# A ViT tower kernel: the pixels' matmuls read x in fp32 instead of two fp16 halves, and x gets two buffers

## What is computed

```
x   = features.reshape(b, c, h, 4, w, 4)
reduce_feats = x.mean((3, 5))                  # mean of each 4 x 4 window
unf = the 16 pixels of each window
q   = layernorm(reduce_feats) @ Wq.T
kv  = layernorm(unf) @ Wkv.T                   # keys and values of 16 pixels
attn  = softmax(q . k over the 16 pixels)      # 8 heads
h   = reduce_feats + (attn . v) @ proj_w.T + proj_b
h   = layernorm(h + lightning_attention(h))    # chunks of 128 tokens, 2 per image
h   = layernorm(h + mixture_of_experts(h))     # top 2 of 8 experts
```

## Time and profile before

| | us |
|---|---|
| median of 3 runs | 3554.83 |
| lowest and highest run | 3554.74, 3558.14 |
| the profiled execution | 3556.12 |
| its span, first to last instruction | 3554.4 |

### The profile page before, as it was taken

One profiled execution on the slowest core, in us unless ns is written; L12 is line 12 of the kernel. 1 busy time (PEld: TensorE's weight loads), 2 busy tenths in 40 slices (PEclk: granted clock), 3 DMA queues, 4 the chain that ended last, 5 costly groups with the idle time before them and its releaser, 6 DMA issues. The chain is left out here.

```text
span 3554.4 us, 81784 instructions
## 1 busy us (share of the span) xinstructions
PE 2747.4 (77%) x22377; PEld 2048.2 (58%) x22377; DVE 2923.7 (82%) x5409; ACT 2049.6 (58%) x12141; POOL 1723.9 (49%) x1661
## 2 busy tenths in 40 slices
PE   3777777777777777777777777777777775399998
PEld 2566666666666666666666666666666655344443
DVE  4999999999999999999999999999999971555554
ACT  3666666666666666666666666666666633244443
POOL 3655555555555555555555555555555520011111
PEclk9999999999999999999999999999999985599999
DMA  2222222222222222222222222222222200000000
GB/s 53 49 49 47 47 47 47 47 47 47 47 47 47 47 47 47 47 47 47 47 47 47 47 47 47 47 47 47 47 47 47 47 1 5 0 16 21 18 21 21
DMA packets 573515, 144.04 MB, mean 41 GB/s; under 512 B 573472, under 2 KB 573472, under 8 KB 573472
## 3 DMA queue, kind: packets, MB, share of 16 engines
q1 hardware_dynamic: 573472, 143.51, 20.6%
HBM read 135.08 MB, written 8.39 MB: 40 GB/s over the span
## 5 line engine op out<-in xcount | busy, mean ns | idle before, releaser
L457 ACT ACTIVATE ps<-ps 128x64 f32<-128x64 f32 x4352 | 935.1, 245 | 848.5 <-PE ps L329 848.3
L607 POOL TENSOR_TENSOR pv<-vs,aw 128x512 f32<-128x512 f32 x512 | 547.1, 1098 | 1178.6 <-DVE aw L781 1178.6
L457 ACT ACTIVATION_READ_ACCUMULATOR ps<-ps 128x1 f32 x4352 | 823.0, 199 | 0.0
L378 PE MATMUL ps<-sm,vpad 128*128 128x128 f32 x4096 | 571.3, 283 | 215.5 <-DVE sm L693 214.6
L378 PEld LDWEIGHTS ps<-sm,vpad 128*128 128x128 f32 x4096 | 511.2, 193 | 303.7 <-DVE sm L693 265.3
L324 PE MATMUL ps<-w_h,xh 128*128 128x128 f16 x2048 | 476.1, 232 | 257.6 <-DVE kq L682 245.7
L329 PE MATMUL ps<-w_h,xl 128*128 128x256 f16 x2048 | 586.7, 286 | 0.0
L327 PE MATMUL ps<-w_h,xh 128*128 128x256 f16 x2048 | 585.3, 286 | 0.0
L324 PEld LDWEIGHTS ps<-w_h,xh 128*128 128x128 f16 x2048 | 237.9, 116 | 492.3 <-issue 348.1
L709 DVE TENSOR_REDUCE agg<-pv 128x128 f32<-128x2048 f32 x128 | 479.6, 3747 | 0.0
L693 DVE TENSOR_TENSOR sm<-ps,decay 128x512 f32<-128x512 f32 x512 | 348.5, 682 | 150.6 <-PE ps L366 150.6
(11 more groups left out here) (222 smaller groups left out, 5971.0 us busy)
## 6 DMA issues: line engine op xcount, KB each, us to landing
xb<-in_x_dram SPq DMA_DIRECT2D x512, 256.0 KB, 4.2
out_dram<-outb SPq DMA_DIRECT2D x128, 64.0 KB, 1.6
w1p<-in_L_ffn_w_dram SPq DMA_DIRECT2D x16, 16.0 KB
b2v<-in_L_ffn_b_dram SPq DMA_DIRECT2D x16, 2.0 KB
w2p<-in_L_ffn_w_dram SPq DMA_DIRECT2D x8, 16.0 KB
b1p<-in_L_ffn_b_dram SPq DMA_DIRECT2D x8, 0.2 KB
sm<-in_L_tok_Wkv_dram SPq DMA_DIRECT2D x4, 16.0 KB, 1.9
w_avki<-in_L_attn_w_qkv_dram SPq DMA_DIRECT2D x4, 16.0 KB, 2.8
```

The costliest lines, as they stand in the source:

```text
L378: mm = nc.tensor.matmul(B7[:, 0:P], vpad[:, s, j * P:(j + 1) * P], sm[:, j * P:(j + 1) * P], start=(j == 0), stop=(j == SL - 1 and s == 0))
L457: return nc.scalar.activation(src if to is None else to, src, ACT.Square, accum_out=dst)
L607: ins = nc.gpsimd.tensor_tensor(pv[:, at].rearrange("p (k d) -> p k d", d=D), vs[:, o, at].rearrange("p (k d) -> p k d", d=D), aw[:, j * W ...
```

## The change

- The tiles `xh`, `xl`, `w_h` and `w_l`, the semaphores `hi_done` and `lo_done`, and all that fills them are gone: `high` on ACT, the subtraction on DVE, the one on POOL, and two set-up instructions on DVE.
- `xb` has two buffers, one for each s.
- A pixel's six fp16 matmuls (four with 128 columns, two with 256) become two fp32 ones, of 128 and 256 columns, with x of `xb` as the stationary operand and `w_ckv` as the moving one.
- `two_pixels(0)` waits for the DMAs of its own unit. `load` waits for `grp` of all units up to two back: PE's last pixel of unit u-2 must be done before x of unit u is fetched.

```
-            xb = sb1("xb", [P, PX])
-            xh = sb1("xh", [P, 2, PX], F16)
-            xl = sb1("xl", [P, 2, PX], F16)
+            xb = sb1("xb", [P, 2, PX])
...
                 def load(i, s):
 
-                    sp.wait_ge(lo_done, done(i, s, 1, 2))
+                    sp.wait_ge(grp, done(i, s, 2, NS))
...
                         if j == 0:
-                            pe.wait_ge(lo_done, done(i, s, 0, 2))
-                            pe.wait_ge(hi_done, done(i, s, 0, 2))
+                            pe.wait_ge(x_in[s], 16 * ST * (i + 1))
...
-                            h, l = xhv[:, n // ST, n % ST], xlv[:, n // ST, n % ST]
-                            nc.tensor.matmul(key, h, w_h[:, 2 * P:3 * P], start=True, stop=False)
-                            nc.tensor.matmul(key, h, w_l[:, 2 * P:3 * P], start=False, stop=False)
-                            nc.tensor.matmul(key, l, w_h[:, 2 * P:3 * P], start=False, stop=True)
-                            nc.tensor.matmul(cv, h, w_h[:, 0:2 * P], start=True, stop=False)
-                            nc.tensor.matmul(cv[:, P:2 * P], h, w_l[:, P:2 * P], start=False, stop=False)
-                            mm = nc.tensor.matmul(cv, l, w_h[:, 0:2 * P], start=False, stop=True)
+                            px = xv[:, n // ST, n % ST]
+                            nc.tensor.matmul(key, px, w_ckv[:, 2 * P:3 * P], start=True, stop=True)
+                            mm = nc.tensor.matmul(cv, px, w_ckv[:, 0:2 * P], start=True, stop=True)
...
-                            at = slice(half * PX // 2, (half + 1) * PX // 2)
-                            nc.scalar.activation(xh[:, o, at], xb[:, at], ACT.Copy).then_inc(hi_done, 1)
...
-                        at = slice(PX // 2, PX)
-                        nc.gpsimd.tensor_tensor(xl[:, o, at], xb[:, at], xh[:, o, at],
-                                                ALU.subtract).then_inc(lo_done, 1)
...
-                        at = slice(0, PX // 2)
-                        V.tensor_tensor(xl[:, o, at], xb[:, at], xh[:, o, at],
-                                        ALU.subtract).then_inc(lo_done, 1)
```

More of the change, by code:

```diff
@@ L102, in vit_tower_kernel @@
         w_ckv = sb("w_ckv", [P, 3 * P])
-        w_h = sb("w_h", [P, 3 * P], F16)
-        w_l = sb("w_l", [P, 3 * P], F16)
         w_qc = sb("w_qc", [P, 2 * P])
@@ L195, in vit_tower_kernel @@
             x_in = [sem("x_in0"), sem("x_in1")]
-            hi_done = sem("hi_done")
-            lo_done = sem("lo_done")
             grp = sem("grp")
@@ L275, in load @@
                 def load(i, s):
-                    sp.wait_ge(lo_done, done(i, s, 1, 2))
+                    sp.wait_ge(grp, done(i, s, 2, NS))
                     for b in range(ST):
-                        sp.dma_start(xb[:, b * PX // ST:(b + 1) * PX // ST].rearrange("p (a w) -> p a w", w=WW),
+                        sp.dma_start(xb[:, s, b * PX // ST:(b + 1) * PX // ST].rearrange("p (a w) -> p a w", w=WW),
                                      xr[bass.ds(i * P, P), s, :, b, :]).then_inc(x_in[s], 16)
@@ L302, in step @@
                     o = 1 - s
-                    xhv = xh[:, s, :].rearrange("p (b k d) -> p b d k", b=ST, d=ST)
-                    xlv = xl[:, s, :].rearrange("p (b k d) -> p b d k", b=ST, d=ST)
+                    xv = xb[:, s, :].rearrange("p (b k d) -> p b d k", b=ST, d=ST)
                     def two_pixels(j):
@@ L474, in pixels_values @@
                                              cvw[:, :, P:2 * P], ACT.Copy).then_inc(cv_done, 1)
[L476 to L480, removed]
-                            at = slice(half * PX // 2, (half + 1) * PX // 2)
-                            nc.scalar.activation(xh[:, o, at], xb[:, at], ACT.Copy).then_inc(hi_done, 1)
                     pixels_values(0)
-                    high(0)
-                    high(1)
                     if there(i, s, 3):
@@ L572, in step @@
                         pool.wait_ge(xs_done, done(i, s, 0, 1))
-                        nc.gpsimd.tensor_tensor(xt[:, 0:PX // 4], xb[:, 0:PX // 4], xb[:, PX // 2:3 * PX // 4], ALU.add)
-                        link(nc.gpsimd.tensor_tensor(xt[:, PX // 4:PX // 2], xb[:, PX // 4:PX // 2],
-                                                     xb[:, 3 * PX // 4:PX], ALU.add))
+                        nc.gpsimd.tensor_tensor(xt[:, 0:PX // 4], xb[:, o, 0:PX // 4], xb[:, o, PX // 2:3 * PX // 4],
+                                                ALU.add)
+                        link(nc.gpsimd.tensor_tensor(xt[:, PX // 4:PX // 2], xb[:, o, PX // 4:PX // 2],
+                                                     xb[:, o, 3 * PX // 4:PX], ALU.add))
                         link(nc.gpsimd.tensor_tensor(xt[:, 0:PX // 4], xt[:, 0:PX // 4], xt[:, PX // 4:PX // 2],
@@ L582, in step @@
                         nc.gpsimd.tensor_tensor(red[:], xp[:, 0, :], xp[:, 1, :], ALU.add).then_inc(xs_done, 1)
-                        pool.wait_ge(hi_done, done(i, s, -1, 2))
-                        at = slice(PX // 2, PX)
-                        nc.gpsimd.tensor_tensor(xl[:, o, at], xb[:, at], xh[:, o, at],
-                                                ALU.subtract).then_inc(lo_done, 1)
                     if there(i, s, 3):
@@ L711, in step @@
                     mask(1)
-                    if there(i, s, -1):
-                        dve.wait_ge(hi_done, done(i, s, -1, 2, -1))
-                        at = slice(0, PX // 2)
-                        V.tensor_tensor(xl[:, o, at], xb[:, at], xh[:, o, at],
-                                        ALU.subtract).then_inc(lo_done, 1)
                     if there(i, s, 2):
```

2 lines of the change are left out of this document (removed).

## The result

The changed kernel takes 4270.64 us (median of 4 runs, 4268.49 to 4274.44); the kernel before, on the same chip, 3554.78 us (3554.61 to 3558.14). The ratio is 1.2011, with a 95% interval of 1.1997 to 1.2025: 20% slower. The forecast was 3960 us and 3710 to 4100. The sign was right; the size was 311 us too small and the range didn't hold the time.

What follows compares the result with a forecast made beforehand. The prediction took a ring through the fetch of x as the bound: 11.2 + 0.2 + 7.0 + 5.15 = 23.55 us, plus 1.9 for the clock, 25.5 us per unit against 22.24, hence 3960 us, range 3710 to 4100.

Steps and rivals of the forecast that it cites:

- DVE and PE bound the kernel before; DVE saves 1.2 us: In the 128 units, DVE looks like the bound with PE close behind; dropping DVE's low half saves some 1.2 us.
- DVE's saving wins: Rival, 6%: x comes early enough, DVE and PE handing over set the pace, 41.5 us per pair of steps, about 3375 us.
- A pair of pixels takes 1.30 us: On PE, two pixels in fp32 take 1.30 us against 0.91 in fp16, 3.1 us more per unit.
- The ring: Once per unit: queries, five pairs with attention, release, fetch of x, window sums, queries; 23.55 us at full clock.
- the strided load: Rival, 5%: PE's strided fp32 stationary operand loads slowly, half a slot more per matmul, 1.74 us a pair, 4230 us.
- release, fetch: From PE's last pixel to POOL's first use of x: 0.2 us for the signal plus 7.0 us.
- window sums to the queries: POOL's window sums, from their start to the start of the query matmul that waits for them: 5.15 us.
- PE, queries to the last pixel, full clock, 1.30 a pair: PE's part from the query matmul to the end of the last pair of pixels: 11.2 us.
- lower clock: PE's clock falls behind its wait at the queries and adds 1.9 us to each unit, giving 25.5 us.
- The wait of 5 us at the queries: PE has 7.2 us of work after the release, sums come after 12.35 us, so PE idles some 5 us.
- The sum: 122 units at 3.26 us more give 398 us, first queries 4, last unit 2: about 3959 us, forecast 3960.
- The ring without the clock loss: Rival, 10%: PE waits at the queries but keeps its clock; 23.55 us per unit, about 3720 us in all.

Runs made afterwards that it cites:

- e3: Changed kernel with x for POOL's sums fetched a second time into its own tile, and 128 neighbouring columns as stationary operand: 3394.07 us, ratio 0.9544.
- e2: Changed kernel with 128 neighbouring columns of x as a pixel's stationary operand in place of every fourth column: 4023.22 us, ratio 1.1313.
- e8: e2 plus eight fp32 matmuls of 256 columns, their result overwritten, ahead of PE's wait for the window sums: 3762.51 us, ratio 1.0576.
- e7: Changed kernel with x sorted in fp32 into neighbouring columns, first half by ACT, second by POOL, load waiting for these copies: 3430.49 us, ratio 0.9644.
- e5: Changed kernel with the stationary operand's columns 8 bytes apart in place of 16: 3979.57 us, ratio 1.1188.
- e10: Changed kernel with the stationary operand's columns 12 bytes apart in place of 16: 4162.86 us, ratio 1.17.
- e9: Changed kernel with the stationary operand's columns 32 bytes apart in place of 16: 4225.3 us, ratio 1.1875.

## Why the prediction missed

**DVE and PE bound the kernel before; DVE saves 1.2 us: right.** Without the two new costs the change gives 3394 us (e3), and the rival "DVE's saving wins" said 3375. By the windows rows DVE is busy for 20.3 us of a unit before (912.04 us of 1000, units of 22.24) and for 19.1 us in e3 (903.41 of 1000, turns of 21.09). The clock rose there as well, from 0.96 to 1.00; no run separates the two.

**A pair of pixels takes 1.30 us: this is the step that failed.** The 0.65 us per pixel came from an fp32 matmul of 384 columns of the earlier trace rows, whose stationary operand `hT` has its 128 columns side by side (`w_avki` is the moving one). Its counting of columns was right (1.31 us in e2), but x is read 16 bytes apart, and then a pair takes 1.97 to 2.07 us. The prediction saw the gap (no fp32 load from a strided view in the trace), named the low bound "no cost" from `attend`, and took that end with 5% for the other. It priced the other end at half a slot per matmul, 0.11 us, 1.74 us a pair; measured it is (1.97 - 1.30) / 4 = 0.17 us per matmul. The upper bound was too low and its chance far too small. In the sum over the ring the term that stood at nothing measured 3.3 us per unit.

**The ring: right in its terms, except the strided load and the clock.** Forecast against one turn, from 2024.10 to 2052.52, one of those in which the clock fell:

| term | forecast | measured |
|---|---|---|
| release, fetch | 0.2 + 7.0 | 7.25 |
| window sums to the queries | 5.15 | 5.12 |
| PE, queries to the last pixel, full clock, 1.30 a pair | 11.2 | 11.3 |
| strided load, four pairs at full clock: 3 x 0.67 + 0.77 | none | 2.8 |
| lower clock | 1.9 | 2.0 |
| sum | 25.5 | 28.5 (28.42 in the trace) |

Between the queries and the last pixel PE waits for nothing, as forecast, though the 1.3 us that the prediction gives ACT's squares there stand in none of its rows.

The third and fifth rows are worked out from PE's 2040.23 - 2024.10 = 16.13 us. The clock's part is the pair at 2024.63 (2.57 against 1.30), the `attend` behind it (2028.76 - 2027.20 = 1.56 against 0.89) and the query matmul (0.53 against 0.43); line 374 has 0.11 more in this turn than on average. The table prices the first pair against 1.30 us and so gives all of its excess to the clock; at full clock the strided load alone makes it 1.86.

The mean turn splits differently. At full clock and with pairs of 1.31 it is 23.83 us (e8; forecast 23.55). The 14 turns of the changed kernel at full clock take 27.09, so the strided load costs 3.3 us over five pairs: 1.86 - 1.31 behind the queries, and 2.8 in the other four. The mean of all 35 turns is 27.89, so the lower clock costs 0.8 us on average, where the forecast had 1.9. That 1.9 was right only for the pairs it assumed (2.1 in e2). The same shows in the mean clock of the units, 0.95 where the prediction said about 0.92.

**The wait of 5 us at the queries: wrong in size, in the main with the same cause.** PE has 9.6 us of work from the release to the wait (2021.32 - 2011.73), not 7.2, so the wait is 2.6 us. The clock falls to its lower level behind it in 21 of 35 turns. In e2, with pairs of 1.31, the wait is 4.0 us: there PE also waits 0.5 us for `keys(2)` on the way (2007.16), which the forecast's 7.2 us left out. DVE, forecast at some 75% busy, is at 69% of the 1000 us, since the unit is longer.

**The sum.** Of the 311 us missed, 122 x (27.92 - 25.5) = 295 us are the unit, 12 us the first queries (the sixth at 151.15, forecast 139), and the rest lies behind the last query matmul (712.0 us after, 705.7 before, forecast 2 more). The experts were untouched, as forecast.

**The rivals.** The strided load was the true one, on top of the forecast's own case, as the prediction had written it: it gave 4230 us against 4271. That it came so near is in part luck. It charged the load 2.2 us per unit and the clock 1.9; they measured 3.3 and 0.8, and the two errors cancel. The range ended at 4100, below it. "The ring without the clock loss" at 3720 us is e8's 3762. The rival's fetch of 5.6 us and less did not come: here the four DMAs need 2.98 us to be issued and land 4.3 us (median of the page) behind their issue. The Trainium skill's fit ("DMA: Bandwidth & Descriptors", "Anatomy of one DMA") is given there for one DMA that GpSimd issues; it does not count SP's time for four, and the prediction's estimate from it did not say so.

## What to carry to other kernels

- When a matmul's operands change type, look at the byte distance between the columns of the stationary one: up to 8 bytes was free here, 16 bytes cost some 0.3 us per fp32 pixel of two matmuls. If the nearest rows of a trace are all contiguous, they are no bound for a strided operand; that end deserves its full price and a real chance.
- An engine that copied data "only" to convert it may also have released the buffer early. Draw the ring of waits that is left when the copy goes, and sum it once around: it told the unit of e2 and e8 to 0.6 us. What a lower clock costs inside the ring has to be worked out anew when another term changes: 2.1 us per unit in e2, 0.8 in the changed kernel.
- Sorting the data on engines with idle time gave both back (e7), once the copy was shared so that neither engine was late.

## What the runs showed of the hardware

- The cost of a strided fp32 weight load grows between 8 and 16 bytes and not beyond: none at 8, about half at 12, full at 16, the same at 32 (e5, e10, the changed kernel, e9), and it vanishes at the lower clock (2.57 against 2.56 us a pair).
- At 16 bytes the loads start 0.23 us apart at full clock, whether their matmul has 128 or 256 columns.
- Behind waits of 2.5 to 2.9 us the granted clock fell to 0.50 in 21 turns of 35 and stayed at 1.00 in the other 14 (changed kernel).
- Eight useless matmuls ahead of a wait of 4 us made the kernel 261 us faster (e8), since the clock stayed at 2.4 GHz.
- ACT's sorting fp32 copy of 128 x 1024 takes 2.08 us, where its contiguous copy to fp16 took 1.08; POOL's sorting product takes 2.92 us, where the contiguous subtraction to fp16 took 2.13.
